# Layer-1 attention: one float32r pack in 64-row halves of the array for row maxima and scores, other loads and another order on TensorE

## What is computed

```python
x = _layernorm(x + _L1_attn_ref(x, ...))
# _L1_attn_ref
q = x @ W_q;  k = x @ W_k;  v = x @ W_v
latent_kv = (k + v) @ W_down_kv                       # width 32
k_rec = (latent_kv @ W_up_k)  by heads;  v_rec = (latent_kv @ W_up_v)  by heads
scores = einsum('bhqd,bhkd->bhqk', qh, k_rec) / sqrt(128)
scores = scores * exp(-0.01 * abs(t_q - t_k))         # decay with distance
out = einsum('bhqk,bhkd->bhqd', softmax(scores), v_rec)
return out @ W_o
```

## Time and profile before

| what | us |
|---|---|
| median of 3 runs (1521.61 to 1532.08) | 1527.86 |
| the profiled execution | 1521.28 |
| its span, first to last instruction | 1519.3 |
| layer 1's attention, first maximum tile to last copy of the sums | 817.9 to 1247.3 |
| layer 1's projections | 750.8 to 806 |

### The profile page before, as it was taken

How to read it: one execution, slowest core, us unless ns; L and a number is a source line. 1 busy time by engine, 2 the same in 40 slices (tenths; PEclk the granted TensorE clock), 3 DMA queues, 4 the chain that set the end, 5 groups by cost and what they waited for, 6 DMA issues and landing times. The chain is left out here.

```text
span 1519.3 us, 23318 instructions
## 1 busy us (share of the span) xinstructions
PE 1289.3 (85%) x7872; PEld 737.0 (49%) x7872; DVE 1135.0 (75%) x1751; ACT 905.5 (60%) x1496; POOL 474.9 (31%) x986
## 2 busy tenths in 40 slices
PE   4298988609999999999753889899999978999998
PEld 1133333407787777878421222222222216777776
DVE  4276666377999999999446768788888835688885
ACT  3188787105555555555341567677777873767774
POOL 4264554003434333333130232243224422121210
PEclk9599999759999999999965699999999997999998
DMA  4524340015666666664256278555754301022200
GB/s 136 118 53 101 62 96 7 5 40 125 153 145 154 146 152 150 148 151 112 94 120 81 51 123 146 108 88 93 119 102 69 58 26 58 1 99 83 83 29 28
DMA packets 72156, 141.09 MB, mean 93 GB/s; under 512 B 13131, under 2 KB 45196, under 8 KB 65132
## 3 DMA queue, kind: packets, MB, share of 16 engines
q1 hardware_dynamic: 71400, 139.13, 43.1%
q10 hardware_dynamic: 648, 0.59, 0.2%
HBM read 121.55 MB, written 16.82 MB: 91 GB/s over the span
## 5 line engine op out<-in xcount | busy, mean ns | idle before, releaser
L1431 ACT ACTIVATE a_PR<-a_ring 128x512 f32<-128x512 f32 x576 | 300.2, 603 | 123.9 <-PE a_ring L1375 123.9
L1443 DVE CUSTOM_DVE_ANT_0 a_junk<-a_mring,a_COR 128x1024 bf16<-128x1024 f32 x256 | 303.9, 1218 | 82.6 <-PE a_mring L1344 82.4
L1318 POOL TENSOR_SCALAR_AFFINE_SELECT a_PR<-a_PR 128x128 f32<-128x128 f32 x512 | 136.7, 297 | 305.6 <-ACT a_PR L1431 305.1
L811 ACT ACTIVATE e_HH<-e_H 128x512 fp32r<-128x512 f32 x184 | 116.4, 633 | 162.5 <-DVE e_H L859 162.4
L1375 PE MATMUL a_ring<-a_QP,a_KP 74*128 74x512 bf16 (+3 forms) x768 | 180.7, 340 | 18.2 <-DMA a_KP<-k_parts 8.3
L415 DVE TENSOR_SCALAR a_PR<-a_PR,a_lo,a_hi 128x1024 f32<-128x1024 f32 (+1 forms) x160 | 122.1, 775 | 78.0 <-ACT a_PR L389 75.3
L389 ACT ACTIVATE a_PR<-a_ring,a_ng 128x1024 f32<-128x1024 f32 (+1 forms) x160 | 155.0, 1033 | 14.9 <-PE a_ring L318 14.1
L1394 PE MATMUL a_OUT<-a_PR,a_V 128*9 128x512 f32 (+3 forms) x1536 | 153.9, 497 | 0.0
L830 DVE TENSOR_TENSOR e_HL<-e_H,e_HH 128x512 fp32r<-128x512 f32 x138 | 140.5, 1018 | 13.3
L1375 PEld LDWEIGHTS a_ring<-a_QP,a_KP 74*128 74x128 bf16 x768 | 57.8, 99 | 176.5 <-ACT a_PR L1431 119.0
L1713 DVE TENSOR_TENSOR e_HL<-e_GL,e_HH 128x512 fp32r<-128x512 f32 x144 | 108.5, 758 | 37.0 <-ACT e_HH L1681 33.5
(11 more groups left out here) (231 smaller groups left out, 2294.6 us busy)
## 6 DMA issues: line engine op xcount, KB each, us to landing
e_ROUTE<-routing SPq DMA_DIRECT2D x24, 704.0 KB
a_QP<-q_parts SPq DMA_DIRECT2D x72, 192.0 KB
e_RAW<-in_w_chunks SPq DMA_DIRECT2D x46, 192.0 KB, 7.6
a_QM<-q_parts SPq DMA_DIRECT2D x64, 128.0 KB, 5.1
e_GATE<-gates SPq DMA_DIRECT2D x8, 1024.0 KB, 4.5
e_ROUTE<-routing SPq DMA_DIRECT2D x8, 640.0 KB
a_KP<-k_parts SPq DMA_DIRECT2D x24, 192.0 KB
e_ROUTE<-routing SPq DMA_DIRECT2D x8, 576.0 KB
```

The source lines that it names most:

```text
L811: nc.scalar.activation(HH[n % NH][:], HT[n % NH][:], ACT.Copy).then_inc(high_done, 1)
L1318: last = nc.gpsimd.affine_select(out=d, in_=d, compare_op=keep, fill=0.0, base=0, pattern=[[step, P]], channel_multiplier=-step)
L1431: nc.scalar.activation(PR[g % NPR][:, j, :], ring[n % NRING][:], ACT.Exp).then_inc(s_read, 1)
L1443: nc.vector.tensor_tensor_reduce(out=junk[:, i % 2, :], in0=mring[k % 2][:], in1=COR[:, c:c + S], scale=1.0, scalar=-3.0e38, op0=ALU.mult, ...
```

## The change

- The packs. q and k are split in two float32r parts instead of three bf16 ones (`PARTS1` = 2). One pack serves maxima and scores: 32 rows of part products and two rows for the maxima per head pair, heads 0 and 1 of a quad in rows 0 to 63, heads 2 and 3 in rows 64 to 127. Rows 32 to 63 of each half are zero for the tiles (GpSimd clears them, `clear`) and ones in K (`set_ones`). `MaxPacks` and the 74-row packs are gone. Loads per half-quad: 4 DMAs of 128 KB for Q, per quad 6 DMAs for K (1 MB), each to every second row. K of quad it+1 is loaded at the start of half 2 it, when the previous half's scores were read.
- `project_l1` makes no third part and no values. It stores only the first quad's heads of the first batch; ScalarE's queue stores the other heads (16 DMAs of 192 KB) at the start of the attention, SP the second batch in halves 1 to 4 (16 DMAs of 256 KB).
- The values are made at the start of `attention_l1` in the score ring, emptied by ScalarE. The decays and the latent lie in `PR`.
- TensorE's order: scores 0 and 1 beside one maximum tile of the other pair of heads, the value product of g-2, scores 2 and 3 beside the second tile, piece by piece in turn. `TILES_BY` sets the tiles: 2 in seven groups of a half, 1 in two. While the first 22 tiles are made, three extra matmuls follow each (`keep_busy`, read by nobody), and 24 after the last.
- Layer 0's attention: each load of 24 rows goes to every third row instead of 24 rows next to each other.

```diff
@@ attention_l0, load
-                        rows = slice(r * 24, r * 24 + 24)
+                        rows = slice(r, PAIRS, NPART)
@@ project_l1
                 for g in range(2):
                     for w in range(NV):
-                        for i, written in enumerate((part1, part2)):
+                        for i, written in enumerate((high_done, low_done)):
                             sp.wait_ge(written, g * NV + w + 1)
-                            store(g, w, i, first_stored)
+                            packs.store(sp, g, w, i, 0, HQ, first_stored)
                 sp.wait_ge(first_stored, 2 * NV * 2 * 16)
-                mp.load_q(sp, 0)
...
+                packs.load_q(sp, 0)
+                packs.load_q(sp, 1)
...
-                def second_part(g, w):
-                    act.wait_ge(rest_done, g * NV + w + 1)
-                    nc.scalar.activation(part(g, w, 1), rest[:, w, g % 2], ACT.Copy).then_inc(part2, 1)
+                def high(g, w):
                     act.wait_ge(val_done, g * NV + w + 1)
...
+                    nc.scalar.activation(parts[:, w, 0, grp(g)], val[:, w, g % 2], ACT.Copy).then_inc(high_done, 1)
...
+                act.wait_ge(first_stored, 2 * NV * 2 * 16)
+                packs.load_k(act, 0)
...
+                            nc.vector.tensor_tensor(parts[:, w - 1, 1, grp(g)], val[:, w - 1, g % 2], parts[:, w - 1, 0, grp(g)].bitcast(F32),
+                                                    ALU.subtract).then_inc(low_done, 1)
@@ module
+HROWS = 64
+TILES_BY = (2, 4, 6, 8, 10, 11, 13, 15, 16)
+NROWS = 2 * PARTS1 * HD
+MAX_ORDER = (2, 0, 3, 1)
@@ class Packs
+    def load_q(self, eng, h):
+
+        it, half = h // 2, h % 2
         b, q, s = it // NQUAD, it % NQUAD, it % 2
...
+        for pair in range(2):
+            heads = slice(q * HQ + pair * 2, q * HQ + pair * 2 + 2)
             for r in range(2):
...
+                rows = slice(pair * HROWS + r, pair * HROWS + NROWS, 2)
+                eng.dma_start(self.Q[s][rows, half].rearrange("r h a t -> r (h a) t").bitcast(F32),
+                              self.QS[heads, :, :, :, tok].rearrange("h a i d t -> (i d) (h a) t")).then_inc(self.q_loaded[s][half], 16)
...
+            for rows, i0, i1 in ((slice(r0, r0 + 32, 2), 0, 2), (slice(r0 + 1, r0 + 17, 2), 1, 2), (slice(r0 + 17, r0 + 33, 2), 0, 1)):
@@ attention_l1, SP
                 for h in range(NHALF):
                     it = h // 2
+                    if h % 2 == 0 and 1 <= it < NIT - 1:
+                        sp.wait_ge(s_read, h * UNITS)
+                        packs.load_k(sp, it + 1)
+                        packs.load_q(sp, h + 3)
+                    if h % 2 == 1 and it + 2 < NIT:
+                        sp.wait_ge(s_read, h * UNITS)
+                        if it + 2 == NQUAD:
+                            sp.wait_ge(stored[1], STORES * 16)
+                        packs.load_q(sp, h + 3)
@@ attention_l1, GpSimd
+                    if 1 <= h < NHALF - 3 and T == (1 if half else KB // 2 + 1):
+                        pool.wait_ge(s_read, h * UNITS)
+                        pool.wait_ge(masked, masked_groups(g - 1) * HQ)
+                        clear(h + 3)
@@ attention_l1, TensorE
+                    last = nc.tensor.matmul(mring[k % 2][:, a:b], QP[s][rows, h % 2, j % 2, var, row * P:(row + 1) * P],
+                                            KP[s][rows, j % 2, var, a:b], start=True, stop=True)
...
+                    last = nc.tensor.matmul(ring[u % NRING][:, a:b], KP[s][rows, j % 2, var, kb * P:(kb + 1) * P],
+                                            QP[s][rows, h % 2, j % 2, var, a:b], start=True, stop=True)
...
+                    score_half(g, 0)
+                    if g >= LAG:
+                        weigh(g - LAG)
+                    score_half(g, 1)
...
+                    tiles = range(issued(g - 1) if g else LEAD, issued(g))
+                    parts_of_unit = list(segments(g % NT, g // NT % 2))
+                    scores = [(n, *piece) for n in (2 * two, 2 * two + 1) for piece in parts_of_unit]
+                    maxima = max_pieces(tiles[two]) if two < len(tiles) else []
+                    for x in range(max(len(scores), len(maxima))):
+                        if x < len(scores):
+                            score_piece(g, *scores[x])
+                        if x < len(maxima):
+                            max_piece(tiles[two], *maxima[x])
...
+                for f in range(NFILL):
+                    values(f)
                 pe.wait_ge(cor_loaded, 32)
...
+                    for piece in max_pieces(m):
+                        max_piece(m, *piece)
...
+                    for n in range(3):
+                        keep_busy(n)
+                for n in range(24):
+                    keep_busy(n)
@@ attention_l1, ScalarE
-                for s in range(2):
-                    act.dma_start(KP[s][PAIRS:PAIRS + 2].rearrange("p j a t -> p (j a t)"), ones16).then_inc(ones_loaded, 16)
...
+                for f in range(NFILL):
+                    keep_values(f)
+                for n in range(STORES):
+                    packs.store(act, n // 8, n % 4, n // 4 % 2, HQ, H, stored[0])
```

More of the change, by code:

```diff
@@ L38 @@
 NPART = 3
+PARTS1 = 2
 PAIRS = NPART * NPART * HD
@@ new lines, in __init__, with store @@
+        self.Q = [sb(f"a1_QP{s}", [P, 2, 2, 2, GW], F32R) for s in range(2)]
+        self.K = [sb(f"a1_KP{s}", [P, 2, 2, S], F32R) for s in range(2)]
+        self.q_loaded = [[sem(f"q_loaded{s}{half}") for half in range(2)] for s in range(2)]
+        self.k_loaded = [sem(f"k_loaded{s}") for s in range(2)]
+    def store(self, eng, g, w, i, h0, h1, done):
+        tok = slice(g * GW, (g + 1) * GW)
+        eng.dma_start((self.QS if w < 2 else self.KS)[h0:h1, w % 2, i, :, tok], self.parts[h0 * HD:h1 * HD, w, i, tok].bitcast(F32))\
+            .then_inc(done, 16)
@@ L1117, in attention_l1 @@
+def attention_l1(nc, t, packs, consts, OD, RD, OC):
     NT = KB + 1
@@ L1170, in masked_groups, with max_head, unit_head @@
         return sum(len(masks(k % NT, k // NT % 2)) > 0 for k in range(g + 1))
+    def max_head(m):
+        return MAX_ORDER[m % HQ]
+    def unit_head(g, n):
+        first = issued(g - 1) if g else LEAD
+        swap = first < issued(g) and max_head(first) < 2
+        return (2, 3, 0, 1)[n] if swap else n
     with ExitStack() as ctx:
         sb, pb, sem = sbuf(nc, ctx), psum(nc, ctx), Sems(nc, ctx)
-        QP = [sb(f"a1_QP{s}", [PAIRS + 2, 2, HQ, 2, GW], BF16) for s in range(2)]
-        KP = [sb(f"a1_KP{s}", [PAIRS + 2, HQ, 2, S], BF16) for s in range(2)]
-        PR = [sb(f"a1_PR{r}", [P, HQ, GW], F32) for r in range(NPR)]
-        COR, ID, V, late, stored = (t[n] for n in ("COR", "ID", "V", "late", "stored"))
+        QP, KP = packs.Q, packs.K
+        COR, ID, PR, stored, cor_loaded, WV = (t[n] for n in ("COR", "ID", "PR", "stored", "cor_loaded", "WV"))
+        V = sb("a1_V", [P, B * KB, VW], F32)
+        lat = PR[0:DL + 1, 2].rearrange("p j c -> p (j c)")
         junk = sb("a1_junk", [P, 2, S], BF16)
@@ new lines, in max_pieces, with max_piece @@
+                def max_pieces(m):
+                    cut = (m // NTILE % 2 * 4 + m % NTILE // HQ + 1) * P
+                    edges = sorted({0, GW, cut, S})
+                    return [(a, b, int(b <= cut)) for a, b in zip(edges, edges[1:])]
+                def max_piece(m, a, b, var):
+                    h, i, k = m // NTILE, m % NTILE, tile_slot(m)
+                    s, row, j = h // 2 % 2, i // HQ, max_head(m)
+                    rows = slice(j // 2 * HROWS, (j // 2 + 1) * HROWS)
+                    if a == 0:
+                        if i == 0:
+                            pe.wait_ge(packs.q_loaded[s][h % 2], (h // 4 + 1) * packs.Q_LOADS)
+                            pe.wait_ge(packs.k_loaded[s], (h // 4 + 1) * packs.K_LOADS)
+                            if h >= 2:
+                                pe.wait_ge(cleared, (h - 1) * 2)
+                        slot_free(k)
+                    last = nc.tensor.matmul(mring[k % 2][:, a:b], QP[s][rows, h % 2, j % 2, var, row * P:(row + 1) * P],
+                                            KP[s][rows, j % 2, var, a:b], start=True, stop=True)
+                    if b == S:
+                        last.then_inc(m_filled, 1)
@@ L1352, in turn, with group @@
                     for part in range(2):
-                        last = nc.tensor.transpose(mring[k % 2][0:2 * NTILE, part * GW:part * GW + P // 2].bitcast(BF16),
-                                                   neg_part[:, part, :], ID[:])
+                        last = nc.tensor.transpose(mring[k % 2][0:2 * NTILE, part * GW:part * GW + P], neg_part[:, part, :].bitcast(F32),
+                                                   consts["ident"][:])
                     last.then_inc(m_filled, 1)
-                def maxima(g):
+                def group(g):
                     for h in range(1, NHALF):
```

340 lines of the change are left out of this document (123 added, 217 removed).

## The result

The changed kernel takes 1587.57 us (median of 3 runs, 1583.82 to 1592.37), 1.040 times the kernel before (95% interval 1.0325 to 1.0471). 1480 was forecast, in a range to 1524. The profiled execution has a span of 1582.1 us, 62.8 more than before. Read against the earlier trace rows the difference has three parts: the first score comes 11.2 us earlier (832.36 against 843.54), the loop from there to the last copy of the sums takes 473.75 in place of 403.15 (+70.6), and the rest +3.4. Of the 11.2 us, 3.9 were there before layer 1's projections began (run 11).

A forecast was written before the change was run, and what follows sets the result against it. TensorE was taken to bound the kernel, VectorE 3.5 us behind per half. Loop -33, start -13.5 and layer 0's loads -1 gave -48 from 1521.3, so 1473, or 1480 as median; range 1448 to 1524 us.

The forecast's parts named there:

- part 1: Order and array halves in layer 1's attention loop: a half takes 23.0 us, the loop 370, that is -33.
- The turn of the maxima, 0.3 a half, as before: Term of the loop's half: TensorE's turn of the maxima costs 0.3 us a half, unchanged.
- part 2: Loads in the loop: K of the next quad has 12.5 us of cover and costs nothing; GpSimd's clears cost nothing.
- The floor of a group: Loop group without tile cost: stays 2.38 us, a half 21.4, set by three PSUM banks and the value product.
- 20 from the order: Share of the loop's -33 us credited to the new order; the other 14 were stalls expected gone.
- Part 3: From projections to first score: first tile about 794, 22 tiles at 1.35 us each, first score 830, -13.5 us.
- rival D: The start stays as long as it is, extra matmuls and late loads eating the projections' gain: 1493 us; chance 0.02.
- Part 4: Layer 0's loads, on the path once before the first matmul: between 0 and -3 us, taken as -1.
- A: Rival in the loop: load and matmul, or the two array halves, take turns; halves of 26.0, 1524 us; chance 0.14.
- B: Slower rival in the loop: turns, each piece costing at least its 0.19 weight load; half 28.8, 1565 us; chance 0.10.
- C: Rival in the loop: K comes late, TensorE stands 4 us in six later quads and loses clock; 1519 us; chance 0.10.
- the list of signs: Signs of being right: full-clock halves of 22 to 24 us, first score at 822 to 838, no K wait in group 5.

The follow-up runs named there:

- run 11: The kernel before with only layer 0's loads of 24 rows going to every third row: 1526.67 us, ratio 0.9997.
- run 1: The changed kernel with GpSimd's clear in the even halves moved from group 5 to group 7: 1557.11 us, ratio 1.0201 to the kernel before.
- run 2: The changed kernel with the turn moved behind the value product and one more tile ahead of it, clear still in group 5: 1528.83 us, ratio 0.9994.
- run 3: The changed kernel with both the clear in group 7 and the turn behind the value product: 1510.6 us, ratio 0.9904 to the kernel before.
- run 5: The kernel of run 3 with the value product put behind the fourth score again: 1507.27 us, ratio 0.9819 to the kernel before.
- run 4: The kernel of run 3 with each tile using the same 64 rows as the scores beside it: 1548.91 us, ratio 1.0148 to the kernel before.
- run 6: The kernel of run 3 with all pieces of a tile issued before the second score of its pair: 1506.24 us, ratio 0.9862.
- run 7: The kernel of run 3 with 50 extra matmuls behind layer 1's projections: 1513.57 us, ratio 0.9926 to the kernel before.

## Why the prediction was wrong, step by step

- **The step that failed** stands in part 1, "The turn of the maxima, 0.3 a half, as before", with part 2's "GpSimd's clears (two per half) stand in groups without masks ... nothing". Before, the fourth score, a value product and three scores of the next group stood between the last tile and the turn. In the change nothing does: the tile belongs to the second pair of scores of group 4, the turn opens group 5, and the chain tile, reading of the tile (1.2), negation, turn lies open on TensorE. That is 1.87 us, and 3.56 where the memset meets the negation. The clear was costed by GpSimd's free time alone, not by what VectorE does in that moment. The clock comes on top: behind 3.56 us at a stand it is at 1.2 GHz for some 9 us, and at the end, behind a stand of 1.87 us and with no tiles left to fill TensorE, until the last copy. Runs 1 to 3 take the parts away. The time falls by 30 without the memset, by 59 without the open chain, by 77 without both; the loop alone by 40, 68 and 77. By the forecast's own sum the loop was to take 370; 473.75 less the 77 is 397.
- **The other 27 us** of the loop are a size in part 1. A half was put at 23.0 = 21.4 + 0.8 + 0.5 + 0.3. Measured without any stall, in the change's order, it is 24.51 and 25.17 (run 3): 1.84 more on average, times 14.6 halves 26.9. The floor of a group is not 2.38 but 2.59. A score costs more at two places of each group, 0.10 until ScalarE can have the first and 0.12 for the fourth, 9 x 0.21 = 1.9 a half where 0.8 stood. At both places the record of its weight load begins with its own (986.81 in run 5), with nothing to hide behind, and that load is 0.18 in place of 0.10 long. The sum had this term, behind the value product, and forgot the second place, behind the wait for a bank. No run separates the longer load from the other type and the other rows. And "20 from the order" was wrong: the order costs 10 (run 5 against 3); the tiles' cost goes because of the array's halves (run 4 against 3). In the kernel before's order, hiding the tiles saves 7 x (2.86 - 2.38) = 3.4 of the longer half's 24.80, the dearer scores take 1.9 back, and the turn's group is some 0.4 longer (991.24 - 988.22 = 3.02 in run 5): 23.7, measured 24.06. Against the average of 24.35 in the earlier trace rows that is a gain of 0.2 a half.
- **Part 3**, the start: values sooner as forecast (first tile 787.63, forecast 794; K's loads no trouble). The tiles were put at 1.35 each. At full clock they are 1.41 to 1.47 apart, at 1.2 GHz with their extra matmuls 2.6. The sum took the full clock, though the trace of the kernel before has 1.2 GHz over the whole of this stretch, windows:

```profile
817.90:843.50 25.60, 12.61 (x64) 2.69 (x64) 24.25 (x45) 0.00 (x0) 0.00 (x0) 0.50 0.74 98
```

There TensorE had time to spare (12.61 busy of 25.60); with the extra matmuls it has none. From VectorE's first product to the first score it took 89.8 us before, 82.5 in the profiled execution of the change, 82.6 in run 3, 91.8 to 93.9 in runs 1, 2, 4, 6 and 7, and 101.9 in run 5, the longer the later the clock came back. So rival D, the start as long as it was, with 2 in 100, was nearer than its chance says. Doing without the extras, worth 12 to 22 us, was not considered.
- **Part 4**, -1, can't be told from nothing (run 11).
- **The rivals.** A and B, in which the two halves of the array take turns, did not occur: run 4 shows what that looks like, 27.1. For the rule that weight loads overlap only across row groups (the Trainium skill, "TensorE: Matmul & The Clock Gate", Part 3, "The mechanism") run 5 has a row at 64: the tile's second piece (985.98) and the third score (986.20) use the same 64 rows and start 0.22 apart, and the score's weight load of 0.18 begins with the tile's piece, at 985.98. That is half of the 0.42 by the rule, so the trace disagrees here too. The short halves of the change, 26.2, equal A's 26.0 by chance: 1.87 of them is the wait. B's own sum comes to 29.2, not 28.8, and would give about 1570. C did not occur: no wait for k_parts stands in the list, and the 8.3 us that TensorE waited for them before are gone. The slow outcome came from a mechanism that no rival had, a wait of TensorE for VectorE, though every part of it could be read from the diff: which group the tile, the turn and the clear are in.
- Wrong too was what the list of signs asked for: halves of 22 to 24 us "at full clock". The clock was taken as given by the loop's business, and no term of the sum had a price for losing it.

## What to carry to other kernels

When work is put in a new order, follow each result to its first reader and count what is left between them on the engine that waits: a turn that had four scores and a value product as cover and now has none cost this kernel's loop 68 us, 29 as a wait (38.1 less 8.7) and most of the rest through the clock. Place an idle engine's chores by what its neighbours do at that moment, not by its own free time. And price a filler before keeping it: here 90 extra matmuls cost more than the slow clock they were put there against.

## What the runs showed of the hardware

- **A memset of GpSimd holds up one kind of VectorE instruction.** The negation (tensor_scalar, float32 from SBUF to SBUF) lasts 1.86 to 1.87 us beside the memset, 12 times of 12 in the change and run 2, and 0.18 elsewhere; the reading of a tile (PSUM and SBUF in) keeps its 1.22 beside the same memset. The Trainium skill, "SBUF — State Buffer", "Who interferes with whom", says that the two engines share a pair of ports as an exclusive lock, which some kinds of VectorE instruction need and which goes to the one that issues first. The end of the negation, 0.04 us after the first memset's each time, agrees with the lock. The order of the records does not: each time the negation's begins 0.03 to 0.04 us before the memset's, and the negation is the one that waits. What the records call a start may come before the lock is asked for; no run shows it.
- **float32r matmuls in the two 64-row halves run side by side**, scores and tiles starting 0 to 10 ns apart where neither waits; in one half they don't (0.34 in run 4).
- **What a stand costs beside itself.** One of 1.5 us cost no clock (run 2); of those of 1.87 eight of 15 did so in run 1 (27.7 against 26.2 for one kind of half, PEclk 0.94) and two of nine in the change, the first and the last; one of 3.56 cost 31.9 in place of the 26.7 that an even half takes with 1.87 and no slow clock (run 1), of which 1.7 are its greater length and 3.5 the clock. At the end of the change's loop the clock did not come back for 55 us, at the start of run 5 not in 60 us in which TensorE was busy 59.78. Windows of run 5:

```profile
790.00:850.00 60.00, 59.78 (x142) 24.09 (x142) 27.97 (x48) 2.58 (x4) 1.21 (x1) 0.50 0.25 77
```

What decides when it comes back stays open: it did so at about 803 in the change's execution, 828 in run 1 and 850 in run 5, in the same code.
